# Four weight quarters loaded once and kept in four buffers, in place of two buffers loaded twice

## The reference

```python
scale = jnp.max(jnp.abs(w)) / INT4_QMAX          # layer 0 ffn, w is kernel, 1024 x 1024 f32
q = jnp.clip(jnp.round(w / scale), -8.0, 7.0)
...
gamma = jnp.mean(jnp.abs(W))                     # layer 1 ffn, W1 and W2, 4096 x 1024 f32 each
return jnp.clip(jnp.round(W / (gamma + EPS)), -1.0, 1.0)
```

## Time and profile before

| what | us |
|---|---|
| median of 2 runs (1600.22 to 1603.07) | 1601.64 |
| the profiled execution, its own time | 1598.37 |
| its span, first to last instruction, core 7 (slowest) | 1596.8 |
| spans of the eight cores | 1570.8 to 1596.8 |
| end of the first block on core 7 (end of L431) | 180.21 |
| end of the first block on core 1 | 160.45 |

### The profile page before, as it was taken

How to read it: one execution, slowest core, us unless ns; L and a number is a source line. 1 busy time by engine, 2 the same in 40 slices (tenths; PEclk the granted TensorE clock), 3 DMA queues, 4 the chain that set the end, 5 groups by cost and what they waited for, 6 DMA issues and landing times. The chain is left out here.

```text
span 1596.8 us, 15349 instructions; the slowest of 8 cores (1570.8 to 1596.8 us)
## 1 busy us (share of the span) xinstructions
PE 1242.8 (78%) x5440; PEld 535.4 (34%) x5440; DVE 419.4 (26%) x704; ACT 475.3 (30%) x550; POOL 90.0 (6%) x97
## 2 busy tenths in 40 slices
PE   0176159996997778755469499979997999889997
PEld 0022024442443223222124144434443444334443
DVE  1398164101323323333275200021002200031000
ACT  3254223334413527546123142013202140031400
POOL 4136100000000000000100000000000000000000
PEclk9988579998998888887789799989998999989999
DMA  9697693002225648779660544333433153231522
GB/s 183 156 169 129 96 148 53 1 1 79 67 66 177 173 128 245 198 224 239 142 106 1 158 139 152 105 132 106 158 120 144 32 153 132 96 115 50 188 106 106
DMA packets 137051, 198.62 MB, mean 124 GB/s; under 512 B 74096, under 2 KB 82320, under 8 KB 132624
## 3 DMA queue, kind: packets, MB, share of 16 engines
q1 hardware_dynamic: 109312, 142.63, 29.6%
q0 software_dynamic: 27664, 55.00, 17.4%
HBM read 199.76 MB, written 33.56 MB: 146 GB/s over the span
## 5 line engine op out<-in xcount | busy, mean ns | idle before, releaser
L1203 PE MATMUL pb<-bigA,wqA 128*128 128x512 bf16 x1024 | 226.2, 379 | 0.0
L1163 PE MATMUL pb<-xn,xbf 128*128 128x512 bf16 x1024 | 222.5, 380 | 0.0
L1146 PE MATMUL pb<-stm,bigB 128*128 128x512 bf16 x640 | 145.7, 390 | 29.4 <-DVE xa_bf L1019 19.2
L1104 ACT ACTIVATE bigA<-pb,biasL,sc 128x512 bf16<-128x512 f32 x128 | 99.5, 777 | 219.9 <-PE pb L1163 219.9
L1185 PE MATMUL pb<-rt,projW 128*128 128x512 bf16 x512 | 125.7, 390 | 40.7 <-DVE rt L1024 35.1
L1054 DVE SCALAR_TENSOR_TENSOR xf<-pb,biasL,xf 128x512 f32<-128x512 f32 x32 | 24.0, 751 | 479.5 <-PE pb L1203 479.5
L1163 PEld LDWEIGHTS pb<-xn,xbf 128*128 128x128 bf16 x1024 | 100.2, 98 | 121.7
L1203 PEld LDWEIGHTS pb<-bigA,wqA 128*128 128x128 bf16 x1024 | 100.2, 98 | 120.8
L1133 PE MATMUL pb<-xn 128*128 128x512 bf16 x320 | 79.5, 416 | 47.7 <-PEq L936 28.1
L684 PE MATMUL pb<-projW,xn 128*128 128x512 bf16 x512 | 112.3, 381 | 0.0
L446 PE MATMUL pb<-rt,idP_s 128*128 128x512 bf16 x112 | 35.2, 445 | 88.4 <-DVE rt L412 88.3
(11 more groups left out here) (128 smaller groups left out, 1008.9 us busy)
## 6 DMA issues: line engine op xcount, KB each, us to landing
xbf<-W1qS SPq DMA_DIRECT2D x128, 256.0 KB, 2.7
wqA<-W2qS SPq DMA_DIRECT2D x32, 1024.0 KB, 4.9
xbf<-W2T SPq DMA_DIRECT2D x23, 512.0 KB, 4.8
stm<-kern SPq DMA_DIRECT2D x8, 1024.0 KB, 10.1
bigA<-W2T POOLq DMA_DIRECT2D x32, 256.0 KB, 10.4
bigA<-W1T POOLq DMA_DIRECT2D x16, 512.0 KB, 12.6
xf<-xT SPq DMA_DIRECT2D x4, 2048.0 KB, 8.9
x1S<-xf POOLq DMA_DIRECT2D x4, 2048.0 KB, 7.8
```

Source lines behind the costliest of these rows:

```text
L1104: got = si(s.activation(bigA[:, fc * 512:(fc + 1) * 512], pb[fc % 2][:, :], AF.Relu, bias=biasL[:, 48 + fc:49 + fc], scale=sc[:, C_Q4:C_Q4 ...
L1146: got = ti(t.matmul(bank[:, :], bigB[:, i * 1024 + ec * 128: i * 1024 + (ec + 1) * 128], stm[:, i * 512:(i + 1) * 512], start=(n == 0), st ...
L1163: got = ti(t.matmul(bank[:, :], xbf[:, (fc % 4) * 1024 + dc * 128: (fc % 4) * 1024 + (dc + 1) * 128], xn[:, p0:p0 + TS], start=(dc == 0), ...
L1203: got = ti(t.matmul(bank[:, :], wqA[:, (dc % 2) * 4096 + fc * 128: (dc % 2) * 4096 + (fc + 1) * 128], bigA[:, fc * 512:(fc + 1) * 512], st ...
```

## The change

The four quarters of `kern` get four buffers of their own: the two halves of `stmF` as before, and the two halves of `xf`. SP issues all four loads at once, without a wait, each on a semaphore of its own; the second pass of loads and its waits are gone. VectorE's maxima and comparisons read the quarter's own buffer.

```diff
+        xfF = xf.ap().bitcast(F32)
+
+        def kq_slot(qr):
+            if qr < 2:
+                return stmF[:, qr * 2048:qr * 2048 + 2048]
+            return xfF[:, (qr - 2) * 2048:(qr - 2) * 2048 + 2048]
+
+        kq_q = [(qsD, sQs), (qaD, sDa), (qbD, sDb), (qcD, sDc)]
+
         @blk.sync
         def _(s):
             for qr in range(4):
-                if qr >= 1:
-                    s.wait_ge(sV, v_qred[qr - 1])
-                q_mx[qr] = qsD(s, stmF[:, (qr % 2) * 2048:(qr % 2) * 2048 + 2048],
-                               kern_quarter_src(qr))
-            for qr in range(4):
-                if qr < 2:
-                    s.wait_ge(sV, v_comb)
-                else:
-                    s.wait_ge(sV, v_cmp(14 * (qr - 2) + 13))
-                qfn = qaD if qr % 2 == 0 else qbD
-                q_cm[qr] = qfn(s, stmF[:, (qr % 2) * 2048:(qr % 2) * 2048 + 2048],
-                               kern_quarter_src(qr))
+                q_mx[qr] = kq_q[qr][0](s, kq_slot(qr), kern_quarter_src(qr))
...
             for qr in range(4):
-                v.wait_ge(sQs, q_mx[qr])
+                v.wait_ge(kq_q[qr][1], q_mx[qr])
                 got = vi(v.reduce_max(
                     sc[:, C_WMX + qr:C_WMX + qr + 1],
-                    stmF[:, (qr % 2) * 2048:(qr % 2) * 2048 + 2048],
+                    kq_slot(qr),
                     axis=AX.X, apply_absolute_value=True))
...
             for qr in range(4):
-                v.wait_ge((sDa if qr % 2 == 0 else sDb), q_cm[qr])
                 for m in range(14):
...
                     got = vi(v.tensor_scalar(
-                        cslot, stmF[:, (qr % 2) * 2048:(qr % 2) * 2048 + 2048],
+                        cslot, kq_slot(qr),
                         sc[:, C_R0:C_R0 + 1], THRS[m], ALU.mult, ALU.is_gt))
```

## The result

The changed kernel takes 1588.39 us (median of 13 runs), the kernel before 1601.93 us on the same chip. The ratio is 0.991, with a 95% interval from 0.9885 to 0.9935: 0.9% less, and the medians differ by 13.5 us. The ratio leaves out the slow runs, those in which the cores of one die show a lower granted clock. The forecast was 1576.3 us in a range from 1563 to 1592. The time lies in the range and the sign is right, but only about half of the 25.3 us came.

The account below looks back on a forecast made before the run. The slowest core's first block, delayed by its front and by GpSimd held up beside VectorE, was taken as what counts. Gains of 15.3 + 10 = 25.3 us took 1598.4 to 1573.1, plus 3.3 for the median: 1576.3 us, range 1563 to 1592.

Parts of the forecast that it names:

- What bounds the first block, and that its end goes into the time: First block: front, units and tail set its end; the slowest core's gain there enters the time one for one.
- Term one: Front of first block: R, when GpSimd goes on with unit 8, moves 66.7 to 51.4, gaining 15.3 us (8.7 to 19.7).
- the front gains less: Rival, chance 0.12: quarters each need 12 us, R is 58, front gains 8.7 us; time 1583 to 1593.
- Term two: From R to the block's end: second-pass loads gone, GpSimd held up less; 10 us, between nothing and 14.6.
- the rival that I gave 0.25: VectorE's chain bounds the first block on all cores: 15.3 + 14.6 = 29.9 us, 1571.7 us; chance 0.25.
- The slower rival: First block: VectorE's early comparisons hold GpSimd up in every quarter; 1603 to 1610 us with R at 58; chance 0.04.
- The rest behind the block: Blocks after the first: unchanged at 1416.6 us, bounds -6 to +3; outside 1408 to 1420 would be wrong.

Follow-up runs that it names:

- x3: Changed kernel with SP's second, third and fourth quarter loads held until all GpSimd's constants have landed: ratio 0.9889 to the kernel before, median 1580.23 us.
- y4: Changed kernel with small constants issued first, the maximum carried through DRAM by SP, and its place ahead of unit 4 instead of 8: ratio 0.9824 to the kernel before.
- z2: y4 with the second value also written and read back by SP instead of GpSimd: ratio 0.9776 to the kernel before, median 1571.89 us.
- y1: The changed kernel run once more without any edit, as a second sample: ratio 0.9931 to the kernel before.
- y3: Changed kernel with GpSimd issuing the seven small constants first on their own semaphore, large ones behind, all quarters still loading at once: ratio 0.9901 to the kernel before.
- x4: Changed kernel with SP instead of GpSimd writing the maximum to DRAM and reading it back, without GpSimd's drain: ratio 0.99 to the kernel before.
- x2: Changed kernel with two unused 1 MB loads of kern added where the second pass had them: ratio 0.9981 to the kernel before.
- z1: Changed kernel with three extra ScalarE passes before units 13 and 19, making GpSimd pause, no load added: ratio 0.9988 to the kernel before.
- x1: Changed kernel with SP's first-pass waits between quarters put back, still without the second pass: ratio 0.9937 to the kernel before, median 1588.65 us.

## Why the prediction was right and wrong

**What bounds the first block, and that its end goes into the time.** Right in kind, but not one for one. The slowest end moved by 15.9 us and the median by 13.5; in x3 it was 19.7 and 21.1, in y4 29.2 and 29.5, in z2 37.3 and 35.4, but in y1 15.3 and 8.9. In the one profiled execution the span fell by only 4.6 us (1596.8 to 1592.2), since its slowest core had a rest of 1427.9 us, above the 1420 that I had allowed.

**Term one, R from 66.7 to 51.4, 15.3 us.** This step failed, and it is the whole of the miss inside the block: R is 62.2 on the slowest core, 4.4 us earlier, outside the bounds of 47 to 58, and 10.9 us short of the term. (Term two gave 1.4 us more than forecast; 2.4 us were lost behind the block.) That the time still lies in the range is thus in part luck: the range had been made wide by other cases. Two sentences of the term were wrong:

1. "The constants that let ScalarE start compete with three more quarters at the start; ScalarE had slack there only as long as units queue up, and the price is within the late end of R." I named the mechanism and did not price it. ScalarE began unit 0 at 36.1 us in the mean over the cores in place of 21.0, so the DMA engines ran out of work, and it began unit 7 at 51.2 to 57.9 us in place of 47.2 to 52.9. (VectorE's first maximum was as late, 33.1 us in place of 17.7, but that did not bind, as y3 shows.) x3 and y3 show it from two sides: with the constants early, the mean R is 55.9 and 56.8, where the two profiles of the changed kernel have 59.4 and 61.6.
2. "Its write issued at 47.4 (the 3.4 us from 57.26 to 60.70)." The 3.4 us were measured where GpSimd had nothing in flight. With units in flight the drain in front of the write lasted 8.9 to 11.1 us in the changed kernel. I had the write stand in its queue behind the units and took its landing from the DMA work; on the chip it was not issued until they had landed. x4 shows it, since from SP it went out in 0.4 us.

Three slips of the prediction change nothing in its sum. SP has three waits in the first pass, not four, and its start has three loads more in a row, not four. And the DMA engines did not run empty in the long issues on core 7 before: their share was 0.72 from 121 to 131 us and 0.51 from 142 to 151 us.

The rival "the front gains less", with R at 58, had the right place and too little of it. Its time, 1583 to 1593, holds the measured one. Its cause, quarters that need 12 us each, was not the one: they landed by about 24 us.

**Term two, 10 us between nothing and 14.6.** Right, and a little nearer its upper end. From R to the block's end core 7 needed 113.5 us before, core 4 needs 102.1 after: 11.4 us. VectorE is the bound on all cores, as in the rival that I gave 0.25; it falls short of 14.6 because the tail behind the last L418 is 12.7 us on core 4 and not core 1's 9.6. The 3.1 us lie in one transfer: from the issue of the last read (1 KB) until VectorE went on it took 5.8 to 6.1 us on cores 2, 4 and 6, and 2.8 us on the other five; why is open. That the two late loads cause the shut-outs, which the forecast offered as half a guess, is shown by x2 and, without any load, by z1.

**The slower rival** did not come. Its rule, shut out in every quarter, is refuted by the counts of the section below. Comparisons back to back did not shut GpSimd out by themselves: a pause of GpSimd went ahead of every shut-out.

**The rest behind the block, unchanged within -6 and +3.** Not quite: its mean over the cores is 1417.8 and 1421.0 us in the two profiles of the changed kernel, against 1414.1 before, but 1413.3 and 1415.3 in x1 and x3, whose blocks end as early. With one profiled execution each, chance isn't excluded for these means. What is regular is this: of the two cores of a pair (0 and 1, 2 and 3, and so on), the one whose block ends later also has the longer rest, in 46 of the 48 pairs of the twelve profiles. What causes it was not tried.

## What to carry to other kernels

Loads that are issued early are not free: ask what small transfer stands in the same engines and who waits for it, and send that one first. A transfer between two engines through DRAM can be carried by an engine that has no other transfers in flight; one from GpSimd waited for all its units before it was even issued. Moved to SP it paid well where the DMA engines were idle (z2), and hardly where they were busy (x4). And a load that looks harmless by its bytes can shift another engine into a bad moment: 2 MB, 7.4 us of DMA work, cost 9 us in the mean end of this block.

## What the runs showed of the hardware that was not expected

GpSimd's shut-out by VectorE's comparisons is narrow and sharp. Over the twelve profiled runs (eight cores each) GpSimd issued 2509 DMAs of units between the start of the first comparison and the end of the last. 47 of them lasted over 5 us (5.96 to 12.35), two more 2.2 and 3.8 us in the same way, two 2.3 us at the very first comparison, and the 2458 others 0.5 to 1.7 us. Every one of the 49 ended 0.12 or 0.13 us behind the end of the quarter's last comparison. Every one came behind a pause of GpSimd of over 3 us and began at least 4.5 us into a quarter. Of the 66 issues of W1 units with such a pause and 4.5 to 11 us into a quarter, 46 were shut out; of the 353 at the same place behind a shorter pause, and of the 48 behind such a pause but earlier in the quarter, none. An issue that begins later has little left to wait for, since a quarter's comparisons last 16.8 us. Issues of W2 units (two DMAs of 256 KB) behind such pauses and in the same part of a quarter were shut out once, in 45. Why this part of a quarter, why so seldom W2, and what lets 20 of 66 through, stays open. No run took the comparisons away or made them another instruction; that it is they that hold GpSimd up rests on the 49 ends.

In "SBUF — State Buffer", section "Who interferes with whom", the Trainium skill says that GpSimd, where it comes second to VectorE in a two-port performance mode, is fully blocked for the whole of VectorE's instruction. The same section puts a DMA that seems to stall beside VectorE down to GpSimd being starved of port time for writing descriptors. No run here shows which mode the comparisons ran in. The trace agrees with the block in that the long issues end with the comparisons; but a comparison lasts 1.28 us, and the long issues waited through four to ten of them, while 2458 took 1.7 us at most beside the same comparisons. Neither a block that ends with each instruction nor one that lasts as long as the comparisons do describes both.
